# Flamingo-style layer pair on one core: token-major SiLU values, one-pass rounding on DVE, four row buffers and the last tokens placed between tiles

## The reference

```python
def act_quant(x):
    scale = 127.0 / jnp.clip(jnp.max(jnp.abs(x), axis=-1, keepdims=True), 1e-05)
    return jnp.clip(jnp.round(x * scale), -128, 127) / scale
...
h = bit_linear(x, w1)                     # rounded x, 512 -> 2048, w1 in -1, 0, 1 times a scale
h = depthwise_conv1d(h.transpose(0, 2, 1), conv_w, conv_b)   # three taps along the tokens
h = h.transpose(0, 2, 1)
h = jax.nn.silu(h)
return bit_linear(h, w2)                  # rounded h, 2048 -> 512
```

## Time and profile before

| | us |
|---|---|
| median of 3 runs | 2201.38 (2200.77 to 2201.7) |
| profiled execution | 2204.66 |
| its span, first to last instruction | 2202.7 |
| DVE busy | 1763.1 (80%) |
| PE busy | 1642.2 (75%) |
| ACT busy | 1581.0 (72%) |
| POOL busy | 578.2 (26%) |

### The profile page before, as it was taken

How to read it: one execution, slowest core, us unless ns; L and a number is a source line. 1 busy time by engine, 2 the same in 40 slices (tenths; PEclk the granted TensorE clock), 3 DMA queues, 4 the chain that set the end, 5 groups by cost and what they waited for, 6 DMA issues and landing times.

```text
span 2202.7 us, 24527 instructions
## 1 busy us (share of the span) xinstructions
PE 1642.2 (75%) x9542; PEld 735.0 (33%) x9542; DVE 1763.1 (80%) x2630; ACT 1581.0 (72%) x1157; POOL 578.2 (26%) x438
## 2 busy tenths in 40 slices
PE   7868766886588578659886888899887566667664
PEld 3212211221122123124343565666564222223221
DVE  6889999999999888958775677777775978787872
ACT  4999999999999999945373444444444567677763
POOL 0000000000000000006121555555553245554543
PEclk9999999999999999979997999999999788888887
...
GB/s 179 1 20 68 20 1 20 67 20 1 1 6 20 44 1 6 6 96 327 199 257 142 68 93 96 96 99 84 80 65 58 24 48 48 48 48 48 39 34 34
DMA packets 104549, 143.65 MB, mean 65 GB/s; under 512 B 8046, under 2 KB 61422, under 8 KB 104050
## 3 DMA queue, kind: packets, MB, share of 16 engines
...
## 4 chain that ended last, share of the span: by engine, by line
ACT 40%; PE 35%; DVE 14%; DMA 5%; issue 3%; POOL 2%; POOLq 0%; SPq 0%; DVEq 0%; ACTq 0%
ACT unit L514 35%; PE psum L1579 5%; PE psum L1613 5%; PE psum L1659 4%; PE psum L1565 4%; DVE hmax_parts L1394 3%; PE psum L1009 3%; PE psum L1015 2%; DMA out_rows<-x3in 2%; DVE unit L423 2%; PE psum L1589 2%; DVE psum L1386 2%; PE psum L1606 1%; DMA xblk<-xnT_scratch 1%; PE psum L1598 1%
## 5 line engine op out<-in xcount | busy, mean ns | idle before, releaser
L514 ACT ACTIVATE unit<-unit 128x4096 f32<-128x4096 f32 x244 | 857.4, 3610 | 0.5 <-DVE unit L423 0.3
L423 DVE TENSOR_SCALAR unit<-feat_proj,text_proj 128x1024 f32<-128x1024 f32 x976 | 667.4, 746 | 66.6 <-PE psum L639 64.7
L639 PE MATMUL psum<-unit,w_pad 128*32 128x512 f32 x3904 | 471.8, 601 | 236.6 <-ACT unit L514 236.6
L639 PEld LDWEIGHTS psum<-unit,w_pad 128*32 128x32 f32 x3904 | 102.2, 109 | 556.9 <-ACT unit L514 399.6
L1659 PE MATMUL psum<-w_q,hidden_q 128*128 128x512 fp8e4 x512 | 144.7, 447 | 77.0 <-ACT hidden_q L1548 39.1
L1637 PE MATMUL psum<-xq_block,w_q 128*128 128x512 bf16 x512 | 140.4, 413 | 45.8 <-ACT hidden L1530 45.4
L1737 POOL TENSOR_TENSOR hidden<-hidden,srow 128x2048 f32<-128x2048 f32 x32 | 144.7, 4524 | 90.4 <-ACT srow L1534 90.4
L680 POOL TENSOR_SCALAR red<-red 128x8 f32<-128x8 f32 x4 | 2.0, 508 | 531.4 <-DVE red L321 531.4
L1518 ACT ACTIVATE psum<-h,conv_b_sb,conv_w_sb 128x512 f32<-128x512 f32 x128 | 98.3, 776 | 47.6 <-DVE h L1380 43.9
L1579 PE MATMUL psum<-xnT_c,wq_sb 128*128 128x256 f32 x512 | 121.7, 392 | 11.0 <-ACT xnT_c L1470 11.0
L547 PE MATMUL psum<-xnT,W_sb 128*128 128x512 f32 x256 | 125.2, 617 | 2.1 <-ACT xnT L465 2.1
...
## 6 DMA issues: line engine op xcount, KB each, us to landing
...
```

The source lines that it names most:

```text
L423: ins = ve.tensor_scalar(units[:, n % 3, k, :], FP[:, bi % 2, k, :], TP[:, k, n:n + 1], None, ALU.add)
L514: ac.activation(units[:, n % 3], units[:, n % 3], ACT.Tanh).then_inc(unit_tanh, 1)
L639: mm = te.matmul(psum[k * TG:(k + 1) * TG, 3 + 2 * grp + half, :], w_pad[:, k, TG - 1 - tt:2 * TG - 1 - tt], units[:, n % 3, k, half * BAN ...
```

## The change

`H2` is laid out [partition, token, chunk]. SiLU writes with a step of 16 values, the two reductions read eight neighbours for each token, and POOL's scaling of a tile goes over one piece of memory, with `srow` repeated along the innermost axis.

Rounding is one DVE instruction that adds and subtracts the magic number and writes bf16. It reads the tile in one piece and writes with a step of 128 values, since `hidden_q` stays [chunk, token]. ACT's `HRA` and `HRB` are gone. A scaling on POOL, from the second tile of a block on, waits for the rounding of the tile before (`h2q_done`).

`x3in` has four buffers with a semaphore each. The loads are still issued two tiles ahead. The steps of the last tokens are cut into four pieces, placed ahead of `OUT` and `W2` of the last block's four tiles, with the SiLU behind the last `SROW`.

The tables of the feed-forward half are new, and a block comes every 391 slots instead of 437; those of attention stay.

```diff
-    H2 = [sb(f"hidden_{r}", [P, HC, BANK], stack=pd) for r in range(2)]
+    H2 = [sb(f"hidden_{r}", [P, BANK, HC], stack=pd) for r in range(2)]
-    x3in = sb("x3in", [P, 2, D], stack=pd)
+    x3in = sb("x3in", [P, 4, D], stack=pd)
...
-    N1, N2, OFF2 = 256, 437, 4330
+    N1, N2, OFF2 = 256, 391, 4330
-    W1 = (248, 257, 267, 285, 305, 321, 393, 413, 428, 444, 457, 528, 538, 628, 666, 675)
+    W1 = (188, 226, 235, 247, 268, 335, 356, 370, 381, 399, 411, 448, 458, 469, 559, 568)
-    HMAX = (536, 742)
+    HMAX = (477, 659)
...
     for f, k, n in at2(q, HMAX):                         # vector_C
-        ve.tensor_reduce(hm[:, k, :], H2[f % 2][:, k * HALF:(k + 1) * HALF, :].rearrange("p c t -> p t c"),
-                         AX.X, ALU.max, apply_absolute_value=True).then_inc(hmax_step, 1)
+        ve.tensor_reduce(hm[:, k, :], H2[f % 2][:, :, k * HALF:(k + 1) * HALF], AX.X, ALU.max,
+                         apply_absolute_value=True).then_inc(hmax_step, 1)
+    for f, i, t in at2(q, HROUND):
+        V.wait_ge(h_scaled, t + 1)
+        V.wait_ge(w2_mm, t - 1)
...
+        ve.tensor_scalar(h2q[:, t % 2].rearrange("p c t -> p t c"), H2[f % 2][:, i * P:(i + 1) * P, :], MAGIC,
+                         MAGIC, ALU.add, ALU.subtract).then_inc(h2q_done, 1)
     for f, i, t in at2(q, OUT):
+        if f == NF - 1:
+            last_tokens(i)
...
-        ac.activation(H2[f % 2][:, c, :], hidden_bank(n), ACT.Silu).then_inc(silu2_done, 1)
+        ac.activation(H2[f % 2][:, :, c], hidden_bank(n), ACT.Silu).then_inc(silu2_done, 1)
...
-    for f, i, t in at2(q, HRA):                          # scalar_C
-        ac.activation(rows, rows, ACT.Copy, bias=MAGIC).then_inc(act_step, 1)
-    for f, i, t in at2(q, HRB):
-        ac.activation(h2q[:, t % 2], H2[f % 2][:, :, i * P:(i + 1) * P], ACT.Copy,
-                      bias=-MAGIC).then_inc(h2q_done, 1)
...
     for f, i, t in at2(q, HS):                           # gpsimd_C
+        if i > 0:
+            G.wait_ge(h2q_done, t)
-        gp.tensor_tensor(H2[f % 2][:, :, cols], H2[f % 2][:, :, cols],
-                         srow[:, cols].unsqueeze(1).broadcast_to([P, HC, P]), ALU.mult).then_inc(h_scaled, 1)
+        gp.tensor_tensor(H2[f % 2][:, cols, :], H2[f % 2][:, cols, :],
+                         srow[:, cols].unsqueeze(2).broadcast_to([P, P, HC]), ALU.mult).then_inc(h_scaled, 1)
...
-            sp.dma_start(x3in[:, t % 2, :], x3_dram[t * P - 1:(t + 1) * P - 1, :]).then_inc(x3in_loaded[t % 2], 16)
+            sp.dma_start(x3in[:, t % 4, :], x3_dram[t * P - 1:(t + 1) * P - 1, :]).then_inc(x3in_loaded[t % 4], 16)
```

More of the change, by code:

```diff
@@ L1168, in flamingo @@
     xqb_loaded = sem("xqb_loaded")
-    x3in_loaded = [sem(f"x3in_loaded_{r}") for r in range(2)]
-    out_stored = [sem(f"out_stored_{r}") for r in range(2)]
+    x3in_loaded, TERN_LOADS = tern_loaded, 16 * PARTS
+    out_stored = [sem(f"out_stored_{r}") for r in range(4)]
     spread_mm, w1_mm, mid_ve, mid_gp, tap0_done, tap_step, silu2_done = (
@@ L1553, in scalar_C @@
             feed_forward(q)
-        A.wait_ge(hmax_step, 3 * NF + 3)
-        ac.activation(acc4[:, :, :], acc4[:, :, :], ACT.Silu).then_inc(silu2_done, 1)
     def tensor_C():
@@ L1661, in feed_forward, with last_tokens @@
                 mm.then_inc(w2_mm, 1)
-        def last_tokens():
-            T.wait_ge(hmax_step, 3 * NF + 4)
-            T.wait_ge(s_step, 4 * NF)
-            te.transpose(psum[0:NB, 7, 0:P], hm4[:, :], ident[:, :]).then_inc(w2_mm, 1)
-            T.wait_ge(hmax_step, 3 * NF + 7)
-            te.matmul(psum[:, 7, 0:NB], hs4[0:NB, 1:2].broadcast_to([NB, P]), ident[0:NB, 0:NB], start=True,
-                      stop=True).then_inc(w2_mm, 1)
-            T.wait_ge(hmax_step, 3 * NF + 9)
-            for c in range(HC):
-                mm = te.matmul(psum[0:NB, 7, :], hq4[:, c, :], w2_q[:, c, :], start=(c == 0), stop=(c == HC - 1))
-            mm.then_inc(w2_mm, 1)
+        def last_tokens(i):
+            if i == 1:
+                T.wait_ge(hmax_step, 3 * NF + 4)
+                T.wait_ge(s_step, 4 * NF)
+                te.transpose(psum[0:NB, 7, 0:P], hm4[:, :], ident[:, :]).then_inc(spread_mm, 1)
+            if i == 2:
+                T.wait_ge(hmax_step, 3 * NF + 7)
+                te.matmul(psum[:, 7, 0:NB], hs4[0:NB, 1:2].broadcast_to([NB, P]), ident[0:NB, 0:NB], start=True,
+                          stop=True).then_inc(spread_mm, 1)
+            if i == 3:
+                T.wait_ge(hmax_step, 3 * NF + 9)
+                for c in range(HC):
+                    mm = te.matmul(psum[0:NB, 7, :], hq4[:, c, :], w2_q[:, c, :], start=(c == 0), stop=(c == HC - 1))
+                mm.then_inc(spread_mm, 1)
         for q in range(QEND):
@@ L1791, in store_rows, with last_rows @@
             skip = 1 if t % TPB == 0 else 0
-            sp.dma_start(out[t * P - 1 + skip:(t + 1) * P - 1, :], x3in[skip:P, t % 2, :]).then_inc(out_stored[t % 2], 16)
+            sp.dma_start(out[t * P - 1 + skip:(t + 1) * P - 1, :], x3in[skip:P, t % 4, :]).then_inc(out_stored[t % 4], 16)
+        ends = slice(SEQ - 1, NTOK, SEQ)
+        def last_rows(i):
+            if i == 0:
+                S.wait_ge(out_stored[0], 16 * NF)
+                sp.dma_start(x3in[0:NB, 0, :], x3_dram[ends, :]).then_inc(x3in_loaded[0], 16)
         def feed_forward(q):
@@ L1813, in sync_C @@
             feed_forward(q)
-        ends = slice(SEQ - 1, NTOK, SEQ)
-        S.wait_ge(out_stored[0], 16 * (NT // 2))
-        sp.dma_start(x3in[0:NB, 0, :], x3_dram[ends, :]).then_inc(x3in_loaded[0], 16)
         S.wait_ge(hmax_step, 3 * NF + 10)
         sp.dma_start(out[ends, :], x3in[0:NB, 0, :]).then_inc(out_stored[0], 16)
-        S.wait_ge(out_stored[0], 16 * (NT // 2 + 1))
-        S.wait_ge(out_stored[1], 16 * (NT // 2))
+        for i in range(4):
+            S.wait_ge(out_stored[i], 16 * (NF + (1 if i == 0 else 0)))
     with nc.Block() as block:
```

140 lines of the change are left out of this document (72 added, 68 removed).

## The result

The changed kernel takes 2250.07 us (median of 4, 2246.3 to 2251.23) where the kernel before takes 2201.07 (2199.58 to 2201.7): ratio 1.0221, 95% interval 1.0203 to 1.0238. It is 49 us slower; the forecast was 37 us faster. The profiled execution took 2250.53 us with a span of 2248.4.

What follows compares the result with a forecast made beforehand. DVE was taken as the bound: a period falls from 58.0 to 54.2 us, seven times -26.8, ramp -10, tail -0.4, total -37. That gives 2164 us, own range 2150 to 2178 (chance 0.48), wider range 2138 to 2194.

Steps and rivals of the forecast that it cites:

- the rounding's price: Four DVE roundings a block, writing with a 256 B step: 1.9 us each taken, range 1.2 to 3.7.
- Rival (d): Rounding loses pairing and pays each hop: 3.7 us each, 2221 us total; slower than before from 3.1; chance 0.10.
- Idle time: DVE's waits per block: 1.5 for PE, 2.0 at taps, 1.2 others, 1.0 for POOL; 5.7 us in all.
- Reduction: Two largest-magnitude passes a block on DVE: 4.4 us each instead of 7.24, saving 5.7 us a block.
- SiLU: ACT's stores with a 64 B step: 0.94 us instead of 0.59, adding 5.6 us a block on ACT.
- rival (b): ACT sets the pace, SiLU taking 1.3 us: about 3 us more a block, 2185 us; chance 0.12.
- Scaling on POOL: POOL's scaling of a tile: 3.7 to 4.5 us, kept at 4.5; waiting for the previous rounding costs nothing.
- Row tiles: Four row buffers: the 12.58 us store no longer holds the reload, so 2.1 us a block goes.
- rival (e): Long store still holds the load behind it, late by up to 3 us in four blocks: 2176 us; chance 0.08.
- Ramp: Block 0's pieces move forward against attention: -10 us, range -5 to -13.
- Tail: Last block's chain 37.6 us instead of 38.0: -0.4, range -4 to +7; gain from moving tokens is given back.
- Rival (c): POOL and DVE exclude each other: three more `MID` a block, 27 us over seven periods, 2191 us; chance 0.08.

Runs made afterwards that it cites:

- a1: Changed kernel with the rounding reading with a 64 B step and writing adjacent values: 2144.1 us, ratio 0.9742.
- b2: Changed kernel with even tiles rounded by lone two-byte writes, odd ones in runs of two values: 2188.0 us, ratio 0.9938.
- a3: Changed kernel with hidden values laid chunk by chunk as before, rounding in one pass with adjacent reads and writes: 2164.8 us, ratio 0.9834.
- b4: Kernel before with one edit, four result-row tiles (`x3in`) instead of two: 2193.6 us, ratio 0.9967.
- b3: Changed kernel with rounding writes in runs of two values, last tokens again behind the last tile: 2133.6 us, against 2125.5 with tokens between tiles.
- d1: Changed kernel without POOL's wait for the rounding of the tile before its scaling: 2260.2 us, ratio 1.0263.

## Why the prediction was wrong, point by point

**The step that failed** is the rounding's price. The prediction had no row of DVE writing with hops, said so, and built its bounds from the reduction's four-byte reads: 1.9 taken, 3.7 the top, for lost pairing and a hop for each value. Measured: 4.72 with the pairing kept, 2.8 more on each of 32 roundings of the fullest queue. What was missing is a cost that no row of the kernel before shows, a two-byte value written alone. L1394's hop of 0.69 ns was a good price for a four-byte read hop (L1505 1.88), not for a four-byte write hop (L1502 2.43). The top of the range wasn't a bound: it was made of the costs that I knew. The larger figure drawn from the Trainium skill ("Vector Engine (DVE) Microarchitecture Reference", Measured stream behaviour on trn2) would have made 2.7, an estimate. That page's table is of four-byte words. For these the trace comes near it (L1502, 2.43), for two-byte ones it doesn't (4.73).

**By the prediction's own sum** 4.82 instead of 1.9 gives 2164+32 x 2.92 = 2257; measured 2250. That this is so near is in part luck, since the same sum is 20 us too long for a1. Rival (d) had the right place and the right sign. Its reason was wrong, a lost pairing, and it was sized at 3.7 and 0.10. It said that the sign changes at 3.1; b2 at 3.10 is still 13 us faster, and it changes at 3.5.

**Idle time.** a1 has the forecast rounding and came out at 2144.1, 20 us under 2164. Its period is 50.5, not 54.2. Busy is 47.9, forecast 48.5; idle is 2.6, forecast 5.7. I had left 1.5 for PE, 2.0 for taps, 1.2 for the rest, 1.0 for POOL. Over a1's seven periods the taps (L1384) waited for nothing and the update for 0.1 us in all; the other 8.6 us of its waits are in the tail. What is left is 6.4 at the reductions, for ACT, and 4.4 at `MID`, for PE. With DVE nearly full, the other engines are ready before it. The 1.0 for POOL shows in a1 as longer roundings, 4 x (2.12-1.90) = 0.9 a block, so that term was right.

The 5.9 us idle of the changed kernel agree with the forecast 5.7 only in size. Over its seven periods the update waits 16.1 us for PE, and PE's product L1662 itself waits 77.6 us for the rounding. That is also why a microsecond of rounding cost more than its length: from a1 to the changed kernel the period grows by 13.5, of which 10.2 are DVE's work and 3.2 new idle time. A slower PE may have a part in this, since the granted clock is 0.79 against 0.88; that wasn't separated, but a3 has 0.81 with 3.3 us idle.

**Reduction**: 4.4 forecast, 4.41 measured. **SiLU**: 0.94 forecast, 1.04 measured; rival (b), ACT paced, is out, since the taps L1384 wait 0.6 us in all for ACT; at the reductions it is 11.9. **Scaling on POOL**: 4.5 taken, 3.68 measured, the low end. **Row tiles**: the wait for DMA is gone in the changed kernel, and rival (e) didn't occur; but the 2.1 us a block that I booked in full were worth 7.3/8 = 0.9 in the old order (b4). **Ramp**: -10 forecast, -8.0 measured.

**Tail.** With 4.73 in its four places my chain of 37.6 becomes 48.9; from 2197.57 to the last store's issue at 2246.18 it is 48.6. The path was right. The lengths agree in part by luck: two scalings in it took 1.6 less than taken, and the four groups of matmuls 1.0 more. The remark that the tokens' gain is given back holds too: b3 measures that gain at 8.1 us, and a1, with the forecast rounding, has a tail of 39.1 against 40.6.

**Rival (c)**, POOL and DVE shutting each other out, is real as a mechanism. In the changed kernel the 54 MIDs since 1740 take 117.6 us where 1.268 each would be 68.5, and ACT waits 43.5 us for them. DVE itself lost little: 32 x (4.82-4.72) = 3 us at the roundings, and 3 more at the first taps (L1384, 0.778 for 0.748 in a1). It doesn't decide the result, because the excluded one was mostly POOL, which has time; d1 turns it round and costs 10 us.
